# Graph, linear attention and experts on 3125 nodes: keys computed once and kept, 32 gather places to the end, the side work dealt out anew

## The reference

```python
xn = layernorm(x)
# edges: the message of an edge is its source's row through the relation's matrix
W = einsum('rb,bio->rio', comp, basis)
agg = segment_sum(einsum('ni,rio->nro', xn, W)[src, edge_type], dst, N)
g = gelu(agg + xn @ loop_w + h_bias + xn)
g = layernorm(g) * ln_gamma + ln_beta
# linear attention over all nodes
query, key = xn @ W_qk[0] + b_qk[0], xn @ W_qk[1] + b_qk[1]
lam = softmax(key, axis=nodes).T @ (xn @ W_v + b_v)
x = x + g + query @ batchnorm(lam)
# experts: the best of 32 for each node
f = layernorm(x); e = argmax(f @ router_w.T + router_b)
x = x + relu(relu(f @ W1[e] + b1[e]) @ W2[e] + b2[e])
```

## Time and profile before

| | us |
|---|---|
| median of 3 runs | 614.11 (612.87 to 617.43) |
| profiled execution | 610.17 |
| its span | 608.3 |
| TensorE busy | 530.1 (87%) |
| DVE, POOL, ACT busy | 381.0, 396.5, 204.8 |
| start of octet 0's matmuls / of the chain / of the last tile's product | 41.33 / 240.97 / 497.87 |

### The profile page before, as it was taken

The page is one execution under the profiler, slowest core; times in us unless marked ns, Lnnn a source line. Parts: engine busy times, 40 slices in busy tenths (PEclk is TensorE's granted clock), DMA queues, the critical chain, the costliest instruction groups (busy, mean ns, idle before and its releaser), DMA issues.

```text
span 608.3 us, 10665 instructions
## 1 busy us (share of the span) xinstructions
PE 530.1 (87%) x3213; PEld 434.3 (71%) x3213; DVE 381.0 (63%) x1427; ACT 204.8 (34%) x406; POOL 396.5 (65%) x409
## 2 busy tenths in 40 slices
PE   0659987999999997997999999999999982389992
PEld 0559965778888996775878787878787861267881
DVE  6879787656545175354566666666666656626884
ACT  6684511120110031155233333333333341155440
POOL 6747777777777460777677777777777710473663
PEclk9979989999999995998999999999999996599996
DMA  8983333333333250344445454545454528474221
GB/s 273 253 264 110 101 95 105 99 107 98 100 106 99 70 183 0 88 129 148 119 132 157 132 155 132 155 132 156 132 155 131 150 72 254 127 209 123 71 96 51
DMA packets 39490, 80.13 MB, mean 132 GB/s; under 512 B 10169, under 2 KB 22394, under 8 KB 39235
## 3 DMA queue, kind: packets, MB, share of 16 engines
q0 software_dynamic: 20048, 55.79, 31.6%
q1 hardware_dynamic: 18372, 22.95, 12.1%
q10 hardware_dynamic: 1008, 0.65, 0.3%
HBM read 66.55 MB, written 12.81 MB: 130 GB/s over the span
## 4 chain that ended last, share of the span: by engine, by line
PE 75%; DVE 12%; issue 4%; DMA 3%; POOL 3%; ACT 1%; DVEq 1%; ACTq 0%; POOLq 0%
PE ps L975 26%; PE ps L1036 14%; PE ps L1025 7%; PE ps L1285 4%; PE ps L1003 4%; PE ps L1012 4%; PE ps L1276 3%; PE ps L1069 3%; POOL both L672 2%; PE ps L1077 2%; PE ps L992 2%; DMA both<-rows_d,inv_i 1%; PE ps L1059 1%; DVE raw_stats L1393 1%; PE ps L1026 1%
## 5 line engine op out<-in xcount | busy, mean ns | idle before, releaser
L626 POOL DMA_INDIRECT gath<-xn_d,src_i x232 | 224.5, 968 | 98.3 <-issue 58.2
L975 PE MATMUL ps<-wmat,gath 128*128 128x80 f32 (+2 forms) x928 | 125.2, 279 | 3.5 <-DVE acc_raw L1542 2.7
L975 PEld LDWEIGHTS ps<-wmat,gath 128*128 128x128 f32 x928 | 118.0, 193 | 14.2 <-issue 8.9
L1463 DVE TENSOR_TENSOR wmat<-hit,wts 128x320 f32<-128x320 f32 (+3 forms) x88 | 50.7, 576 | 115.7 <-PE ps L975 115.4
L626 POOL DMA_INDIRECT acc_raw<-xn_d,src_i x96 | 97.1, 1012 | 35.6 <-issue 25.0
L1489 DVE TENSOR_TENSOR acc_raw<-acc_raw,ps 128x80 f32 (+3 forms) x352 | 74.5, 253 | 34.6 <-PE ps L975 33.2
L975 PE MATMUL ps<-wmat,acc_raw 128*128 128x128 f32 (+2 forms) x480 | 67.3, 288 | 1.4 <-ACT acc_raw L734 1.4
L975 PEld LDWEIGHTS ps<-wmat,acc_raw 128*128 128x128 f32 x480 | 62.1, 197 | 6.3 <-issue 2.4
L1036 PE MATMUL ps<-wk_et,acc_raw 128*128 128x256 f32 (+1 forms) x200 | 52.2, 385 | 0.0
L1036 PE MATMUL ps<-wq_wv,acc_raw 128*128 128x256 f32 (+1 forms) x200 | 52.0, 384 | 0.0
L672 POOL DMA_INDIRECT both<-rows_d,inv_i x25 | 24.1, 964 | 40.5 <-DVE inv_i L1840 33.2
(11 more groups left out here) (247 smaller groups left out, 816.9 us busy)
## 6 DMA issues: line engine op xcount, KB each, us to landing
rows_d<-both SPq DMA_DIRECT2D x24, 256.0 KB, 2.2
gath<-xn_d,src_i POOLq DMA_INDIRECT x232, 2.8
both<-in_x SPq DMA_DIRECT2D x24, 128.0 KB, 3.4
both<-in_x SPq DMA_DIRECT2D x4, 640.0 KB, 9.6
xn_d<-both SPq DMA_DIRECT2D x4, 640.0 KB
acc_raw<-in_w_t SPq DMA_DIRECT2D x1, 2080.0 KB
acc_raw<-in_w_t SPq DMA_DIRECT2D x1, 2048.0 KB, 7.1
acc_raw<-xn_d,src_i POOLq DMA_INDIRECT x96, 2.8
```

Source lines behind the costliest of these rows:

```text
L626: g.indirect_dma_start(place_of(n), None, table, bass.IndirectOffsetOnAxis(ap=src_i[:, n:n + 1], axis=0)).then_inc(done, 16)
L975: ins = t_.matmul(bank[:, m * w:(m + 1) * w], place_of(n)[:, m * P:(m + 1) * P], wmat_tiles[:, k, 0:w], start=k == pair[0], stop=k == pair ...
L1463: d.tensor_tensor(made, hit[:, :, 0:width(q)].unsqueeze(2).to_broadcast([P, w, B, width(q)]), wts[:, :, cut].rearrange("p b t -> p t b").u ...
```

## The change

- The keys are computed once, two tiles a piece, 13 pieces in octets 0 to 3 (`KEYS_AT`) into four PSUM banks. ACT copies each to accumulator tiles 7 to 13 (`keep`, L814), DVE takes the running maximum of the copies (`take_max`, L1553 and L1556). After octet 3 the maxima are joined, transposed and spread over all partitions as a shift (`join_max`, `turn_top`, `make_shift`, `shift_rows`). DVE adds the shift to the kept keys in place (`lower`, seven instructions in octets 4 to 7), ACT takes the exponential in place, and `weigh` follows, five tiles an octet, in octets 5 to 9.
- The dense steps stand in octets 4 to 11 (`DENSE_AT`), the cross product in 12 and 14, small algebra in 10 to 13. The chain starts in octet 15 and has one tile an octet up to 36, then one in 38 and one in 42. The cross product is added in octet 25.
- The gather places stay 32: from octets 20, 21 and 26 on, three banks of eight lie in accumulator tiles 0 to 5, which the chain has read by then (POOL waits for that).
- Octet 3 is gathered from raw `x` too (`RAW` = 4). `judge`, the codes and the first dense build stay in octet 3. Clears, waits for them, loads of the bases and of `x`, and the routing of one tile move accordingly.

```diff
+KEYS_AT = {(0, 1): 0, (0, 2): 1, (0, 3): 2, (1, 1): 3, (1, 2): 4, (1, 3): 5, (2, 1): 6, (2, 2): 7, (2, 3): 8,
+           (3, 0): 9, (3, 1): 10, (3, 2): 11, (3, 3): 12}
+LOWER_AT = {(4, 3): (0, 1), (5, 1): (2,), (5, 3): (3,), (6, 1): (4,), (6, 3): (5,), (7, 1): (6,)}
+DENSE_AT = [(4, 2), (5, 0), (5, 2), (6, 0), (6, 2), (7, 0), (7, 2), (8, 0), (8, 1), (8, 2), (9, 0), (9, 1), (9, 2),
+            (10, 0), (10, 1), (10, 2), (11, 0), (11, 1), (11, 2), (11, 3)]
-STARTS = list(range(19, 43))
+STARTS = list(range(15, 37)) + [38, 42]
-RAW = 3
+RAW = 4
 def place_of(n):
-    if n >= EARLY * OCT:
-        return gath[:, n % OCT, :]
...
+    q, k = divmod(n, OCT)
+    bank = q % 4
+    if bank == 3:
+        return gath[:, k, :]
+    first = 2 * bank if q >= EARLY + (bank == 2) * 6 else UPPER + 2 * bank
 def gather(n):
-    if n < EARLY * OCT:
-        if n >= STAGE:
-            pool.wait_ge(multiplied, n - STAGE + 1 + OCT)
-        done = landed[n % STAGE // PAIR]
-    else:
-        pool.wait_ge(multiplied, n + 1)
-        done = gathered[n % OCT]
+    if n >= STAGE:
+        pool.wait_ge(multiplied, n - STAGE + 1 + OCT)
+    done = landed[n % STAGE // PAIR]
 # POOL, in an octet
+    if q in (EARLY, EARLY + 1, EARLY + 6):
+        pool.wait_ge(once.pre_done, 2 * (q % 4) + 2)
 # ACT, in an octet, behind raw_normalise(q + 1)
+    for w in range(4):
+        if (q, w) in KEYS_AT:
+            keep(KEYS_AT[q, w])
 # DVE, in an octet
-    add_edges(q, 0, bases)
-    if q == RAW:
-        judge()
-        dense_codes()
-        dense_build(0)
-    dense_step(q, 0)
...
+    for w in range(OCT // PAIR):
+        add_edges(q, w, bases)
+        dense_step(q, w)
+        before_it = (q, w - 1) if w > 0 else (q - 1, OCT // PAIR - 1)
+        if before_it in KEYS_AT:
+            take_max(KEYS_AT[before_it])
+            if KEYS_AT[before_it] == PAIRS:
+                join_max()
+        if w == 1:
+            middle(q, beside)
+        for g in LOWER_AT.get((q, w), ()):
+            lower(g)
+def middle(q, beside):
+    if q == JUDGE:
+        judge()
+        dense_codes()
+        dense_build(0)
+    if q + 1 < RAW:
+        raw_statistics(q + 1)
+        raw_scale(q + 1)
+def take_max(k):
+    v.wait_ge(kept, k + 1)
+    if k == 0:
+        d.tensor_copy(highest, key_double(k)).then_inc(max_done, 1)
+    else:
+        d.tensor_tensor(highest, highest, key_double(k), ALU.max).then_inc(max_done, 1)
+def keep(d):
+    act.wait_ge(keyed, d + 1)
+    s.copy(key_double(d), key_bank(d)[...]).then_inc(kept, 1)
```

More of the change, by code:

```diff
@@ L456, in edge_schedule @@
         def edge_schedule(octet):
[L460 to L474, removed]
[L475 to L488 removed]
+            for q in range(GOCT):
+                octet(q, BESIDE.get(q, "chain" if q >= CHAIN0 else ""))
+        def place_of(n):
+            q, k = divmod(n, OCT)
[3 more added lines that the diff above has]
+            first = 2 * bank if q >= EARLY + (bank == 2) * 6 else UPPER + 2 * bank
+            at = k * NPAD + first * P
             return acc_raw[:, at:at + D]
@@ L600, in _ @@
             load_basis(1)
+            sp.wait_ge(m_mult, 1)
+            load_basis(0)
+            sp.wait_ge(dense_mult, NDENSE + 2)
+            for t in range(3):
+                load_x(sp, t, once)
             for t in range(NT):
@@ L755, in _, with octet @@
             raw_normalise(0)
-            def octet(q, beside, i):
+            def octet(q, beside):
                 if q + 1 < RAW:
@@ L1125, in to_rows, with piece @@
                 ins.then_inc(done, 1)
-            def piece(q, quarter, beside, i):
-                if quarter % 2 == 1 and 0 <= 2 * (q - DENSE0) + quarter // 2 < NDENSE:
-                    dense_product(2 * (q - DENSE0) + quarter // 2)
+            def piece(q, quarter, beside):
+                if (q, quarter) in KEYS_AT:
+                    keys(KEYS_AT[q, quarter])
+                if (q, quarter) in DENSE_AT:
+                    dense_product(DENSE_AT.index((q, quarter)))
+                if WEIGH0 <= q < WEIGH0 + NT // WEIGHED and quarter > 0:
+                    first = WEIGHED * (q - WEIGH0)
+                    for t in ((), (0,), (1, 2), (3, 4))[quarter]:
+                        weigh(first + t)
+                if (q, quarter) in CROSS_AT:
+                    cross(CROSS_AT[q, quarter])
@@ L1163, in piece @@
+                elif beside == "max_last" and quarter == 1:
+                    turn_top()
+                    turn_router()
+                elif beside == "max_last" and quarter == 3:
+                    shift_rows()
                 elif beside == "sum_last" and quarter == 2:
@@ L1203, in chain, with octet @@
                     product(t, 0, KD * B, once)
-            def octet(q, beside, i):
+            def octet(q, beside):
                 for quarter in range(4):
                     edges(q, quarter)
-                    piece(q, quarter, beside, i)
+                    piece(q, quarter, beside)
             edge_schedule(octet)
@@ L1548, in first_stats, with lower @@
+            def lower(g):
+                v.wait_ge(kept, PAIRS + 1)
+                v.wait_ge(shift_turned, 2)
+                n, count = rows(4 * g), min(4, NT - 4 * g)
+                place = key_group(g).rearrange("p (j k) n -> p j k n", k=KD)
+                shift = ps_mix[0][0:n, 0:D].rearrange("p (k n) -> p k n", k=KD).unsqueeze(1).to_broadcast([n, count, KD, P])
+                d.tensor_tensor(place, place, shift, ALU.add).then_inc(lowered, 1)
             def first_stats(t, c):
@@ L1777, in _ @@
             finish_row(NT - 2, once)
-            route(NT - 3, once)
             first_stats(NT - 1, once)
```

342 lines of the change are left out of this document (156 added, 186 removed).

## The result

The changed kernel takes 625.87 us (median of 4 runs, 624.37 to 627.49); beside it the kernel before took 613.49 (606.33 to 617.43). The ratio is 1.024, with an interval of 1.015 to 1.034. The forecast was 605.6, in a range of 592 to 615. Medians are of all runs; the ratios leave out the runs that lie over 1.5% above the fastest of their kernel. The profiled execution takes 624.37 us, with a span of 622.4.

What follows compares the result with a forecast made beforehand. TensorE's work was taken as the bound, with POOL's gathers ending the edge stage after the change. Accumulator complete near 490 instead of 497.87 gains 8.5 us, tail unchanged: 601.7 profiled, 605.6 on the median's scale; range 592 to 615.

Steps and rivals of the forecast that it cites:

- Keys once, 26 us off TensorE: Separate key pass for the maximum and the shift's matmuls go: 27 us off TensorE, about 1 back, net 26.
- The loop in octets 0 to 3: Statistics, normalising, ACT's copy, DVE's maxima and adds follow each other: 13.2 us an octet where 9.43 stood.
- The bounds of the maxima: DVE's maxima in octets 0 to 3: 0.60 to 0.69 us each, bounds 0.58 and 1.03, moving an octet -0.3 or +1.0.
- Octet 4: Behind judge, codes, dense build, last maxima, joining: second quarter at 93 us, transposes at 97.5, octet 5 at 102.
- Octets 5 to 14: Work of 100.9 us plus waits, 6 of them in octets 10 and 11: about 111, octet 15 near 213.
- The small chain behind lam: Small operations in the small algebra, which left TensorE 3.30 us idle before: about 2.7 us of wait stay.
- POOL ends the stage: POOL waits until 251.5, last gather at 482.8, accumulator complete near 490; TensorE alone ready 6 us sooner; gain 8.5 us.
- The tail unchanged: Rank and experts after the accumulator stay at 110.4 us; one routing step less there costed at nothing.
- The rival "slower": Octets 1 to 4: TensorE starves 3 us an octet, clock drops, up to 5 us an octet more: 620 us; chance 0.12.
- One sign of being wrong: Among the signs against the forecast: a granted clock below 0.9 over 41 to 102 us.
- Slow gathers: Gathers beside twelve two-SBUF-input maxima: no cost by the skill page, up to 5 us by the trace; sum unchanged either way.
- the rival "the gain is eaten": Gathers after octet 21 slowed by DVE's long operations, 0.4 us per octet instead of 0.11: 6.7 us, 612; chance 0.20.

Runs made afterwards that it cites:

- e1: Changed kernel with, on DVE, the dense sum ahead of the weight build and dense builds two steps ahead: 611.5 us, 0.998 of the kernel before.
- e2: Changed kernel with two of an octet's three key copies on ACT ahead of the normalising steps, the third in their middle: 618.54 us, ratio 1.013.
- e3: Changed kernel with the judging of the bases moved from octet 3 to octet 14: 621.93 us, 1.017 of the kernel before.
- e4: Changed kernel with the lower gather places only from octets 24 to 26 on, upper tiles cleared in 21 to 23: 628.02 us, ratio 1.026.
- e7: Changed kernel with the last two tiles' first products (early) moved from octets 42 and 43 into 40 and 41: 621.16 us, ratio 1.018.
- e6: Changed kernel with the edits of e1, e2, e3, e4 and e5 together: 587.25 us, 0.965 of the kernel before.
- e8: Changed kernel with the edits of e6 and those of e7 too: 580.74 us, 0.954 of the kernel before.
- e5: Changed kernel with DVE's small algebra behind lam moved from the end of octet 12 to its middle: 614.03 us, 1.007 of the kernel before.
- e10: e8 with the cross product added in the middle of octet 24 instead of at the start of octet 25: 579.26 us, 0.943 of the kernel before.

## Why the prediction was wrong

- *Keys once, 26 us off TensorE:* not measured by itself. It is borne out indirectly, since with e1 octet 15 comes at 212.84 where the sum of work and waits said 213. That they agree so closely is in part luck, for the waits are others than those forecast: 3.8 us in the ring for 6, and 1.75 for ACT's exponential, which the sum did not have.
- *The loop in octets 0 to 3:* right, 12.8 us a turn against 13.2, and e2 shows the cause. The bounds of the maxima held: 0.68 us each.
- *Octet 4:* right (93.27 and 97.46 against 93 and 97.5); e3 shows that judging is 2.8 us of it.
- *Octets 5 to 14:* **this is the step that failed.** I weighed DVE's work in an octet against TensorE's and allowed 6 us for octets 10 and 11. I did not follow one dense step through both queues. What bounds is not the work but the ring, which costs in octets 5 to 9 too (10.7 us, put at nothing): 19.6 us of waits for 6, and slow clocks behind some of them. The 6 was low by its own prices too: with 1.7 and 0.5 a step beside 4.0, three and four steps are 10.6 and 12.8 us of DVE's time, not 9.5 to 10, which against TensorE's 6 to 7 would have given some 10; 8.9 were measured there. e1 gives 17.4 us of it back by order alone. What it needed was in the order of the two engines' instructions: on DVE the sum stands behind a weight build that waits for a later piece of TensorE than the one that needs the sum.
- *The small chain behind lam:* right, 3.53 us of wait for 2.7. From L1133 to octet 14 TensorE ran at the lower level. Most of that price was in the sum, without being named: the 10.3 us for the small algebra come from a stretch at 0.81, with the same eight records at 3.78.
- *POOL ends the stage:* the times came out as worked out (e1: 482.90 for 482.8, 490.80 for 490), but the reason was half of it, so that the match at 490 is in part luck. TensorE alone was put 6 us sooner; at its lower clock in octets 40 to 42 it isn't (e4), and its waits for gathers in octets 39 to 43, named as a sign of being right, are absent. Both end there together (e4, e7, e6 against e8).
- *The tail unchanged:* wrong in the profiled executions, 3.8 us longer in the changed kernel and 7.4 in e1; the cause stays open. Of the 3.8, some 2.8 pass from the last tile's first product to its logits (L1080), 12.9 us instead of 10.1: its products run at the lower clock. In e1 a stretch 60 to 70 us behind the accumulator has a clock of 0.69 besides, where the changed kernel has 1.00. But no rest of the change explains it: e2, e4 and e6 leave the same rest of 2.24 before these products, which take 1.93 there, and their tails are 111.4, 114.7 and 111.4. The kernel before has a rest of 1.70 less than 1 us ahead of them (the lines below). So the tail's clock differs from execution to execution in work that no edit touches. In e1's profiled execution the accumulator is complete 7.1 us sooner than in the kernel before, and the tail takes it back.
- *The rival "slower":* it had a chance of 0.12 and the wrong place. The mean clock does fall, to 0.81 over octets 3 and 4, yet they start where the loop alone put them; the mechanism that made the kernel slower was none of my rivals. One sign of being wrong did come: the clock over 41 to 102 is 0.89, under the 0.9 named, where the kernel before has 0.97.
- *Slow gathers:* the rival "the gain is eaten" did not happen. From octet 21 on POOL kept its pace.

TensorE at the last tile's products, first in the kernel before, then in e4:

```profile
497.11 0.60 PE L1059 MATMUL ps<-rwt,both 128*128 128x32 f32 x4 [1.70 <-DVE oh_sum L1600]
...
497.87 1.93 PE L1036 MATMUL ps<-wk_et,acc_raw 128*53 128x256 f32 x8
```

```profile
513.65 1.93 PE L1057 MATMUL ps<-wk_et,acc_raw 128*53 128x256 f32 x8 [2.24 <-DVE acc_raw L1489]
```

## What to carry to other kernels

Where two in-order engines hand work to and fro, compare not their loads but the ring: write down for one item what stands ahead of it on each engine, and for each of those what it waits for. If one of these waits for something later than the item itself, the ring is serial, and an order that hands the item over first can be worth a good part of the work saved (here 17 us, beside the 26 worked out for the keys). When a removed wait shows nothing, a second bound may lie within a few us of it, and both must go in one run. A stretch that is made light for TensorE is not free: fill it with work from its neighbours, or its clock may fall for what follows (0.85 against 1.00 here). And one execution's clock is no proof: compare the same records in several kernels that share them.

## What the runs showed of the hardware

A rest of 1.66 us (after one of 0.55 some 20 us earlier) was followed by 13 us at the lower level, 1.2 GHz: `early` took 3.70 us instead of 1.92, although TensorE was busy throughout. Its stretches in the changed kernel before and after that rest (columns as above, the clock third from the end):

```profile
460.00:478.80 18.80, 17.16 (x123) 15.00 (x121) 14.50 (x68) 4.76 (x9) 14.20 (x16) 1.00 0.45 138
...
480.00:493.00 13.00, 13.00 (x51) 10.62 (x49) 5.20 (x27) 0.97 (x1) 9.91 (x11) 0.50 0.40 116
```

I had counted on rests of about 3 us only. The same place is slow in all seven kernels that leave the light octets as they are (3.70 us in five, 2.76 in e3, 3.22 in e5, after rests of 1.66 to 1.82), and at 1.92 in the four that fill them (e7 to e10).

Elsewhere the same rest was not always followed by the lower level. Behind the 3.53 us ahead of L1133 the records took 3.78 us in the changed kernel, e1, e2 and e4, and 1.99 in e3 and e7. Behind 2.23 or 2.24 at the last tile they took 3.66 in the changed kernel and e1, and 1.93 in e2, e4 and e6. What decides between them no run shows.

Under a maximum of two SBUF tiles that still had 0.3 us or more to run, a gather that began took longer: 1.20 us at 57.41, 1.31 at 70.21 and 1.15 at 86.01, against 0.95. These are all three such cases in the changed kernel; gathers that began in a maximum's last 0.16 us took 0.95 to 0.98.

```profile
57.41 1.20 POOL L628 DMA_INDIRECT acc_raw<-xn_d,src_i  x1 [0.30 <-issue]
...
70.21 1.31 POOL L628 DMA_INDIRECT acc_raw<-xn_d,src_i  x1 [0.30 <-PE ps L985]
```

It is not the maxima alone. Of the changed kernel's gathers from 41 to 505 us, the 25 that began with 0.3 us or more of a maximum, a weight build (L1464) or a dense build (L1527) to run took 1.27 us in the median, and the 277 that began beside none of them 0.95.

The Trainium skill ("SBUF — State Buffer", section "Who interferes with whom") infers that such a DVE operation doesn't hold up a gather's descriptors, though it contends with GpSimd's reads. The trace shows that a gather beside a maximum does take longer, by 0.2 to 0.4 us, at most 1 us in all for the 12 maxima. A gather reads its row numbers (`src_i`) in SBUF; no run tells whether that reading or the descriptors are held up.
